# A Mamba-like scan on TensorE: the second token half of each state's sum one place earlier in the written order

## The reference, cut to what matters

```python
def step(state, inp):
    x_t, dt_t, k_t, q_t = inp
    dtv = jax.nn.sigmoid(dt_t + dt_head_b)
    dtv = dtv / (1.0 + dtv * jnp.sum(k_t * k_t, axis=-1, keepdims=True))
    kk = k_t * k_t
    state = state * (1.0 - dtv[..., None] * kk[:, None, :]) + (x_t * dtv)[..., None] * k_t[:, None, :]
    y_t = jnp.einsum('bdn,bn->bd', state, q_t)
    return (state, y_t)
y = jnp.transpose(ys, (1, 0, 2)) + D * x
y = y * jax.nn.silu(z)
```

## Time and profile before

| what | value |
|---|---|
| median of 3 runs | 1814.18 us |
| the profiled execution's own time | 1818.58 us |
| its span, first to last instruction | 1816.8 us |
| TensorE matmuls busy | 1669.8 us (92%) |
| VectorE busy | 1469.6 us (81%) |
| GpSimd busy | 1370.2 us (75%) |
| ScalarE busy | 1315.2 us (72%) |
| mean granted TensorE clock | 0.981 of full speed |
| first and last read-out of the scan start at | 141.2 us and 1391.7 us |

### The profile page before, as it was taken

How to read it: one execution, slowest core, us unless ns; L and a number is a source line. 1 busy time by engine, 2 the same in 40 slices (tenths; PEclk the granted TensorE clock), 3 DMA queues, 4 the chain that set the end, 5 groups by cost and what they waited for, 6 DMA issues and landing times.

```text
span 1816.8 us, 34000 instructions
## 1 busy us (share of the span) xinstructions
PE 1669.8 (92%) x12301; PEld 1439.4 (79%) x12301; DVE 1469.6 (81%) x3084; ACT 1315.2 (72%) x2689; POOL 1370.2 (75%) x644
## 2 busy tenths in 40 slices
PE   6879999999999999999999999997777999999998
PEld 5768787887878888787887878786666888899997
DVE  3648889898988989898898989888987678766663
ACT  3567878888787888879788887876643855666664
POOL 0009899999999999999999999999997343444443
PEclk9999999999999999999999999999987999999999
DMA  5011112212211221221122212212212444455552
GB/s 198 1 59 53 60 65 76 83 53 83 77 60 66 86 73 54 83 76 63 62 87 71 64 72 77 71 62 85 76 63 90 116 132 101 117 140 140 139 136 28
DMA packets 69463, 149.79 MB, mean 82 GB/s; under 512 B 5936, under 2 KB 43312, under 8 KB 68912
## 3 DMA queue, kind: packets, MB, share of 16 engines
q1 hardware_dynamic: 57008, 130.84, 20.9%
q0 software_dynamic: 12288, 16.79, 5.4%
HBM read 121.91 MB, written 17.30 MB: 77 GB/s over the span
## 4 chain that ended last, share of the span: by engine, by line
PE 62%; DVE 13%; ACT 13%; issue 6%; POOL 4%; DMA 0%; DVEq 0%; ACTq 0%; POOLq 0%
PE po L1844 10%; PE ph L1844 9%; PE pD L1130 8%; DVE room L1179 7%; PE pY L1147 7%; PE pA L731 6%; POOL room L1188 3%; PE pB L926 3%; PE pB L936 3%; PE pB L1226 3%; ACT room L1160 2%; PE pA L722 2%; PE pB L957 2%; PE pB L942 2%; PE pA L652 1%
## 5 line engine op out<-in xcount | busy, mean ns | idle before, releaser
L1198 POOL TENSOR_TENSOR room<-room 128x1024 f32<-128x1024 f32 x256 | 609.2, 2380 | 154.0 <-DVE room L1113 133.8
L1179 DVE TENSOR_TENSOR_SCAN room<-pD,last,room 128x256 f32<-128x256 f32 x1024 | 688.7, 730 | 38.7 <-PE pD L1130 25.6
L1188 POOL TENSOR_TENSOR room<-room 128x1024 f32<-128x1024 f32 x256 | 608.6, 2378 | 47.4 <-PE pY L1147 47.3
L1160 ACT ACTIVATE room<-room,kkT 128x512 f32<-128x512 f32 x512 | 359.8, 716 | 57.7 <-PE pD L1130 56.4
L1130 PE MATMUL pD<-fixed,room 128*128 128x128 f32 x2048 | 320.6, 280 | 67.0 <-DVE room L1179 57.5
L1147 PE MATMUL pY<-fixed,room 128*128 128x128 f32 x2048 | 319.5, 280 | 14.8 <-POOL room L1188 14.8
L1130 PEld LDWEIGHTS pD<-fixed,room 128*128 128x128 f32 x2048 | 242.0, 144 | 98.9 <-issue 50.1
L1147 PEld LDWEIGHTS pY<-fixed,room 128*128 128x128 f32 x2048 | 249.2, 145 | 67.0 <-POOL room L1188 30.9
L343 POOL DMA_INDIRECT xg<-xn_rows,W x64 | 67.6, 1056 | 196.7 <-DVE W L337 181.4
L1803 ACT ACTIVATE h<-ph 128x512 f32<-128x512 f32 x128 | 76.7, 599 | 137.6 <-PE ph L1844 137.6
L1844 PE MATMUL po<-w_up,h_up 128*128 128x256 f32 x512 | 149.5, 292 | 3.2 <-DVE h_rest L1711 2.6
(11 more groups left out here) (315 smaller groups left out, 3418.0 us busy)
## 6 DMA issues: line engine op xcount, KB each, us to landing
room<-kq_rows SPq DMA_DIRECT2D x128, 512.0 KB, 3.7
w_in<-w_d SPq DMA_DIRECT2D x32, 1024.0 KB, 5.7
room<-ndS SPq DMA_DIRECT2D x16, 512.0 KB, 3.2
xt<-x_in SPq DMA_DIRECT2D x16, 256.0 KB, 2.9
y_out<-xo SPq DMA_DIRECT2D x16, 256.0 KB, 2.1
xn_rows<-xnC SPq DMA_DIRECT2D x16, 256.0 KB, 2.2
W<-weights SPq DMA_DIRECT2D x1, 1808.0 KB, 9.2
W<-weights SPq DMA_DIRECT2D x1, 1697.5 KB, 16.8
```

The source lines that it names most:

```text
L1160: act.activation(decT[:, m % 2, t, :], turn2(ndT, it, NT * DI, t * DI, DI), ACT.Copy, bias=1.0, scale=turn2(kkT, it, NT * DS, t * DS + m, ...
L1179: dve.tensor_tensor_scan(run, pD[h][:, k2 * TB:(k2 + 1) * TB], run, last[:, bass.ds(later(it) * (DS * DT) + m * DT + k, 1)], ALU.mult, ALU ...
L1188: pool.tensor_tensor(sq[:, m % 2], st[:, m % 4], kqb[:, m % SLOTS, 1, :].unsqueeze(1).broadcast_to([P, DT, TB]), ALU.mult).then_inc(sem("r ...
L1198: pool.tensor_tensor(st[:, m % 4], turn2(u, it, DT * TB).rearrange("p (k t) -> p k t", k=DT), kqb[:, m % SLOTS, 0, :].unsqueeze(1).broadca ...
```

## The change

The second half of each state's sum is written at place 23+4m instead of 24+4m, and the opening product of the second half (`open1`) at place 23 instead of 24. The first half stays at 22+4m. No instruction is added or removed, no wait is changed, and the sums add up in the same order.

```diff
-    rows_d=42, turn_d=74, mod_d=75, score=79, scores=81, dec=11, sum=22, open0=21, open1=24, dec_t=6, saved=21,
+    rows_d=42, turn_d=74, mod_d=75, score=79, scores=81, dec=11, sum=22, open0=21, open1=23, dec_t=6, saved=21,
...
-            piece = nth(n, "sum", 2)
-            if 0 <= piece < 2 * DS:
-                m, t = piece // 2, piece % 2
+            for t in range(NT):
+                m = nth(n - t, "sum", 4)
+                if not 0 <= m < DS:
+                    continue
                 if t == 0:
                     pe.wait_ge(sem("read_out"), it * DS + m + 1)
                 for k in range(DT):
```

## The result

The changed kernel takes 1854.95 us (median of 4 runs, 1852.87 to 1855.7). The kernel before took 1815.01 us in the same comparison (median of 4, 1814.15 to 1821.28). The ratio is 1.0212 (95% interval 1.0199 to 1.0225), 39.9 us more. The direction and the mechanism were right. The size was not: 1854.95 us lies above the forecast of 1845.5 and outside the range, which ended at 1851.

A forecast was written before the change was run, and what follows sets the result against it. TensorE was taken to lead, its idle time in waits coming back to its own earlier work. Five loops (30.4 us) plus turn 15 (1.3) gave +31.7 onto 1814.2: 1845.9, said as 1845.5 us, range 1829 to 1851.

The forecast's parts named there:

- the prediction's own signs of being wrong: Turn staying near 79 us, one of five TensorE waits not growing, or a regular-turn clock below 1.00.
- Items 1 to 4: Delayed pieces L631, L585, L936, L957 at places 27, 35, 51, 55: +0.44 us each a turn, in 14 turns.
- Item 2: Place 35, L585: ScalarE and TensorE end together before L926, so +0.44 us a turn, perhaps 0.02 less.
- item 4's wait: Place 55, L957: through ScalarE and VectorE, TensorE's 1.04 us wait for a bank grows by 0.44.
- Item 5: Place 3 of the next turn, L722, awaited by VectorE: +0.44 us a turn, at the least 0.39.
- The number of occurrences: Items 1 to 4 in 14 turns each, item 5 in 13: 69 times 0.44 = 30.4 us.
- item 1: Place 27, L631: ScalarE idle for it, then TensorE awaits its decay; +0.44 us in each of 14 turns.
- Behind turn 15: In turn 15 VectorE waits longer for TensorE's counts L199 behind moved sums: +1.3 us, bounds 0 and 2.
- The clock: TensorE's longer waits before VectorE's scans leave the full clock, judged by the end of turn 14: costed at 0.
- The rival that I gave 0.05: Clock falls once a turn behind the longer stand before 762.59: 14 to 28 us more, about 1867; chance 0.05.
- The execution's own time: Profiled execution of the kernel before lay 4.4 us above the median; that difference was put onto the median, giving 1814.2.
- GpSimd: Read-out stops waiting for the sum, gain costed at 0; wait at the block's start grows from 1 to some 6 us.

The follow-up runs named there:

- e1_five: Against the kernel before: second half of the sum one place sooner only for states 1, 3, 7, 8 and 11; 1852.71 us, ratio 1.0201.
- e2_rest: Against the kernel before: second half sooner only for the other eleven states, and `open1` at place 23; 1816.47 us, ratio 0.9997.
- e5_only1: Against the kernel before: second half sooner only for state 1, past L631 at place 27; 1821.52 us, ratio 1.0024.
- e3_after_fill: The changed kernel with 16 idle TensorE transposes at place 7 of turns 2 to 14, in its 1.94 us wait; 1850.59 us, ratio 1.0188 to the kernel before.
- e8_only11: Against the kernel before: second half sooner only for state 11, past L722 at place 67; 1823.01 us, ratio 1.0028.
- e4_before_fill: The kernel before with 12 idle TensorE transposes at place 7, nothing reordered; 1816.78 us, ratio 1.0003.
- e10_four: Against the kernel before: second half sooner only for states 1, 3, 7 and 8, without state 11; 1844.74 us, ratio 1.0146.
- the five single ratios: Five kernels against the kernel before, each moving the second half of one state only (1, 3, 7, 8 or 11); ratios 1.0024, 1.0033, 1.0033, 1.0019, 1.0028.
- e12_firsts_d: Against the kernel before: decay turns at places 27, 51 and 55 put behind L631, L936 and L957; 1804.22 us, ratio 0.9931.

## Why the prediction was right in kind and 9 us short

The sum was 31.7 us onto 1814.2 us. In the profiles it is 37.1, 5.4 more. Another 3.6 us of the miss lie in how the profiled execution stands to the median, and 0.4 in rounding 1845.9 down. Two of the prediction's own signs of being wrong came true: the clock in regular turns fell below 1.00, and one of its five waits, that of 1.04 us, didn't grow.

**The mechanism, right.** The order changes only "where another stage's piece W stands at the same odd place", "W starts later by one second half of a sum": e1_five has the whole loss and e2_rest none.

**Items 1 to 4, right to 0.03 us.** Each was put at 0.44 and measured 0.41 to 0.43 alone, 1.73 together. Item 2 rested on a tie, and it held. Only the place of item 4's wait was wrong: "the bank for which TensorE stood 1.04 us" was to grow to 1.5. It stayed at 1.04, and a new 0.50 us stands at L714, which needs the same square L803 that VectorE waited for. TensorE and VectorE both move by the 0.44, so their distance doesn't change.

**Item 5, too large.** "+0.44, at the least 0.39, since TensorE's start of L722 was also just held by VectorE". It measured 0.28. The hold was worth more than the 0.05 us that I took it for. Counted from the turn of the decay ahead of it (756.72 and 1103.49), L722 starts 0.41 us later, but VectorE has its result only 0.31 us later. Before, L722 began 0.05 us after `og` was ready and its matmuls took 1.99 us; after, `og` had been ready for 0.46 us and they took 1.89. So 0.13 us of the sum ran in time in which L722 was held or slow anyway. No run separates the two.

**The number of occurrences, a little too high.** Items by occurrences were to give 30.4 us. The turns have 1.7 + 24.4 + 1.7 = 27.8. Of the gap, 0.16 a turn is item 5, and item 1 costs turn 1 nearly nothing (0.04 us in e5_only1's profile, though the wait itself grows there too).

**Behind turn 15, too small.** 1.3 us was the term, with 2 as its upper bound. It measured 1.9 + 1.0 = 2.9. From turn 15 to the first gather the profiles have 139.6 to 142.4 us in the kernels with none or one of the five items, 141.0 in the kernel before, and 143.9 to 145.3 in those with four or five. So the term is there, but one profile gives it no closer than a few us. What of it are the counts isn't separated.

**The clock, the step that failed.** "So I cost the clock at 0." It rested on one row, the full clock at 1232 us with TensorE busy 2.58 of 4 us. That was a single case with less idle time than the one that the change made: at 781 us TensorE is busy 2.03 of 4 us, and 0.63 of the full clock follows. In its place the runs showed +4.3 us in the regular turns, and 4.2 of them went when the wait was filled (e3_after_fill). It is the term with no price that is shown to belong to the change: with 4.3 us for it the forecast would have been 1849.8, inside the range. The Trainium skill ("TensorE: Matmul & The Clock Gate", section "What's actually happening") has the throttle as the default and activity as what releases it. By that rule the longer wait could halve the clock, and here the trace agrees with the rule against my reading, in 8 turns of 12. The rival that I gave 0.05 had the event and its cause right ("behind the longer stand before 762.59") and its price wrong: 14 to 28 us against 4.2 us. A clocked turn is only 0.4 to 0.8 us longer (81.47 to 81.83 against 81.07), though TensorE is busy 1.2 us longer in the one of 81.73, since part of the longer work falls into TensorE's own short waits behind it: those of 0.11 and 0.14 us before L645 and a turn of the decay, and the one of 0.29 us for GpSimd at 1124.90, stand in the clean turn and not in this one. In e8_only11 a low stretch costs 0.67 us in its turn and 0.19 in the next.

**The execution's own time.** "The difference goes onto the median" put all of the 4.4 us by which the profiled execution before lay above the median on the account of that execution. After, the profiled execution lies 0.75 us above its median. That is 3.6 us of the miss. Another 3.0 us stand ahead of the first moved instruction, less 1.0 at the experts. Neither is shown to belong to the change: both lie inside what these parts vary by between the profiles, and e1_five starts at 148.10 and still has its median within 2.3 us of the changed kernel's. The 4.4 us of the kernel before's profile have the same kind of source: its experts took 422.6 us, and those of e4_before_fill 419.2. So about 5.6 of the 9.4 us are scatter between executions, which neither speaks for nor against the mechanism. The errors of the sum in part cancel, too: loops 2.6 us too high, behind turn 15 1.6 too low. The kernel before itself had medians of 1815.01, 1818.05, 1817.73 and 1816.09 us in the four comparisons, and against 1818.05 the loss of e1_five is 34.7 us.

**GpSimd, right in effect and wrong in form.** Its earlier read-out brought nothing, as costed. But no wait of 6 us came at the block's start. Its idle time is now in pieces of at most 2.5 us.

The terms, forecast against profile: loops 30.4 against 27.8, behind turn 15 1.3 against 2.9, clock 0 against 4.3, ahead of the first moved instruction 0 against 3.0, experts 0 against -1.0. That makes 31.7 against 37.0.

Open stays how much of turn 15 and 16 is the clock's (the filled kernel won 4.2 us in the regular turns and was 2.0 us longer than e1_five from turn 15 to 16, where e10_four without filler was longer too), and why the five single ratios add to 1.37% where the five together have 2.01%. The clock explains little of it, since e8_only11 has its own low stretches: from turn 2 to 14 the five single profiles add to 27.5 us where the changed kernel has 28.7. Behind turn 15, up to the first gather, they add to -0.4 us against 2.9; the rest is in the scatter of five intervals of 0.1% each.

## What to carry to other kernels

In streams of written order, price a reordering place by place: the piece that moves back costs its full delay each time its consumer already stands idle for it and TensorE later stands for that consumer, such loops add up, and the pieces that move forward win nothing if nobody on the path waits for them. The same list of idle consumers, read the other way, gives the improvement: the waited-for pieces ahead of the unwaited ones took 0.7% off here. Where a change lengthens one of TensorE's waits, put the granted clock of the stretch behind it among the terms, priced by what its later waits absorb and not by the lost cycles.

## What the runs showed of the chip

- A wait of 1.94 us in a TensorE stream that is busy 93% of the turn was followed by the low clock in 8 of 12 regular turns (changed kernel) and in every third turn (e8_only11); a wait of 1.64 us at the same place never was in a regular turn, in the kernel before, e10_four and e12_firsts_d. So the same wait at the same place may or may not cost the clock, and turns of 81.83 and 81.07 us follow one another in one execution.
- 16 transposes that nobody uses, put into that wait, kept the clock at 1.00 in all regular turns and did not lengthen the turn (81.08 us, e3_after_fill).
